# A fused decoder's last stage: TensorE transposes the probabilities ahead of the queries and keys, and GpSimd's inverse root is cut at another place

## The chip, the cores and the metric

One Trainium2 chip, one core of it. The metric is the device time of one launch in microseconds (us), the median of several runs. The kernel is written instruction by instruction: each engine (TensorE, VectorE, ScalarE, GpSimd and SyncE, which starts the transfers) has its own queue, works through it in order, and waits on semaphores that other engines raise.

## The reference, cut to what matters

The program is a decoder of four blocks, twelve parts in all, on x of shape 4 x 256 x 128. Each part adds to x what it makes of a layer norm of x. The change lies in the twelfth part, `L3_ffn`, a small transformer of its own with six layers, sixteen heads of 64 and attention in windows of 32 rows:

```python
def attn_layer(x, Wqkv, qs, ksc, Wo):
    q, k, v = split(x @ Wqkv)                   # 128 -> 3 * 1024
    q = l2norm(q) * qs;  k = l2norm(k) * ksc    # per head: t / max(norm, 1e-12)
    q = q * cos * scale + rotate_half(q) * sin * scale
    k = k * cos * inv + rotate_half(k) * sin * inv
    out = local_attention(q, k, v)              # softmax over 64 or 96 keys of a window
    return out @ Wo
def ffn_layer(x, g, b, W1, b1, W2, b2):
    xn = (x - mu) / sqrt(var + 1e-05) * g + b
    a, gate = split(xn @ W1 + b1)
    return a * gelu(gate) @ W2 + b2
for i in range(6):
    x = attn_layer(shift_tokens(x), ...) + x
    x = ffn_layer(shift_tokens(x), ...) + x
```

## The kernel before

The last stage is one block of code, `stream`, that overlaps everything. A **job** is one layer for one of the four batches: 24 jobs. A job has eight **groups**, each a pair of heads: 192 groups. Time goes in **ticks**, `for s in TICKS`, one group per tick. Every engine's queue is written as such a loop, and in tick `s` each does for the group `g = s - lag` (or `s + lead`) what its stage of the pipeline asks for. So the order of the work is fixed by where a step stands in the body of the loop, and by its lag.

In one tick TensorE does, in this order:

- one or two of the q, k and v products of a later job, 128 x 512 each (L2078, or L2087 and L2091);
- the scores of group `s` (L2100 lays the window's mask, L2108 multiplies). They wait for the turned queries and keys, `net_qk_T`, and for the exponentials of the group before;
- the **turn** (L2120): four transposes of `net_rope`, the queries and keys of group `s + 1`, into a bank of PSUM. It waits until GpSimd has scaled them (L2348), and until the turn before has been copied;
- the **flip** (L2129): four transposes of the probabilities of group `s - 2`. It waits until GpSimd has divided them by their sums (L2335), and until the flip before has been copied;
- a step that comes once a job (output projection L2141, shifts L2151 to L2153 and L2161, the feed-forward part L2170 to L2207);
- the values (L2226): probabilities of group `s - 3` times v.

VectorE, per tick: the reciprocal of the sums of group `s - 1` (L2405), the maxima of the scores of group `s` (L2409), two products of the rotation (L2373, L2379) that read a bank of PSUM, the copy of the flip (L124, `net_probs_turned`), and in odd ticks the copy of the turn (L124, `net_qk_T`; ScalarE has the even ones). In even ticks it sums squares (L2445) after the flip's copy. Once a job there are the layer norm's sums, its root (L2391 to L2399) and two residual adds (L2453, L2487). ScalarE does the exponentials, squares and further copies.

GpSimd, per tick: it divides the probabilities of group `s - 1` (L2335), scales group `s + 2` with its head norms (L2348), and adds the two products of the rotation (L2327). TensorE's flip and turn of one tick thus wait for the same tick of GpSimd, the flip for its first operation, the turn for its second.

Every four ticks comes the inverse root of the head norms, `inverse_root`: fourteen operations on 128 x 32 numbers (a start value of two operations, three Newton steps of four), each waiting for the one before it. It is cut in two lots. The **early** lot, `EARLY_OPS` operations, stands at the end of one tick (`PROJ + 5`), after the add. The **late** lot stands in the next tick (`PROJ + 6`) between the division of the probabilities and the scaling that uses its result:

```python
if j is not None:
    inverse_root(pool, head_sums[:, j % 2, :], 1e-24, head_inv[:, j % 2, :], head_temp, rooted, ROOT_OPS * j, False)
g = s + SCALE
if 0 <= g < G:
    ...
    pool.wait_ge(rooted.sem, rooted.at(0, ROOT_OPS * (j + 1)))
```

Twice in a job there is such a pair of lots. Once a layer GpSimd also makes the tables of the next layer (L2315, L2319).

## Time and profile before

| what | us |
|---|---|
| median of three runs | 2811.66 (2810.72 to 2820.9) |
| the profiled execution, its own time | 2823.85 |
| its span, first to last instruction | 2822.1 |
| busy: TensorE, VectorE, ScalarE, GpSimd | 2514.6, 1779.7, 1535.3, 1364.0 |
| the last stage, about | 1811 to 2820 |
| from one job to the next inside it | 39.83 (40.61 where a layer begins) |

The profiled execution took 12 us more than the median of the others. In the last stage TensorE is busy for 765.19 us of the 800 us from 1909 to 2709, at the full granted clock (1.00); GpSimd for 638.83 us, VectorE for 639.19 us, ScalarE for 567.11 us. The page's chain of work that ended last has 21% of the span on TensorE, 8% on GpSimd and 4% on VectorE. A job is the unit to read: all of them from the second on look alike to within some hundredths of a microsecond.

### The profile page before, as it was taken

The numbers are of one execution on the slowest core, as the hardware profiler recorded it, in microseconds if no ns is written. First come the engines' busy times: TensorE is split into PE (matmuls) and PEld (weight loads), VectorE is DVE, ScalarE is ACT, GpSimd is POOL, SyncE is SP. The second block draws the span as 40 slices with busy tenths as digits, with TensorE's granted clock in tenths as the row PEclk, the third lists the DMA queues.
The fourth block names the chain that finished last, engine by engine and source line by source line (L and its number), as shares of the span: only waits on it lengthen the run. The fifth ranks groups of instructions, "written<-read, shape, count | busy, mean of one in ns | idle before, by whom it ended". The sixth has DMA issues, their size and how long they took to land. (4 is left out here: it accounts for less than half of the span.)

```text
span 2822.1 us, 57927 instructions
## 1 busy us (share of the span) xinstructions
PE 2514.6 (89%) x20585; PEld 1603.7 (57%) x20585; DVE 1779.7 (63%) x4074; ACT 1535.3 (54%) x4979; POOL 1364.0 (48%) x1981
## 2 busy tenths in 40 slices
PE   6899978988989988978559999789999999999997
PEld 3555544645655655645444555356666666666665
DVE  4566665545656755555564555577887787878784
ACT  1455534722756755633224555357766776777664
POOL 0344442401536633320003444388877887788772
PEclk8899997998998999999768999899999999999998
DMA  3000000010000010000010000101010101101000
GB/s 71 1 1 1 1 9 1 2 34 15 2 5 1 2 34 1 1 7 1 8 29 1 1 1 1 55 17 39 20 47 20 35 24 32 35 24 47 20 26 7
DMA packets 45711, 47.85 MB, mean 17 GB/s; under 512 B 11947, under 2 KB 31413, under 8 KB 45430
## 3 DMA queue, kind: packets, MB, share of 16 engines
q1 hardware_dynamic: 45430, 44.18, 5.7%
q8 instruction: 167, 2.74, 0.4%
q14 instruction: 114, 0.93, 0.1%
HBM read 31.05 MB, written 0.52 MB: 11 GB/s over the span
## 5 line engine op out<-in xcount | busy, mean ns | idle before, releaser
L1033 DVE TENSOR_REDUCE negmax<-scores 128x1 f32<-128x508 f32 (+4 forms) x512 | 212.5, 467 | 213.8 <-PE scores L918 182.6
L1013 POOL TENSOR_TENSOR l_xattn_probs<-l_xattn_probs,rowinv 128x512 f32<-128x512 f32 x128 | 130.4, 1040 | 421.1 <-DVE rowinv L1025 421.1
L2273 ACT ACTIVATE net_probs<-bank,net_negmax 128x96 f32<-128x96 f32 x768 | 251.7, 341 | 105.1 <-DVE net_negmax L2409 104.0
L1013 POOL TENSOR_TENSOR lora_probs<-lora_probs,rowinv 128x508 f32<-128x508 f32 (+1 forms) x256 | 149.6, 618 | 247.3 <-DVE rowinv L1025 247.3
L2327 POOL TENSOR_TENSOR net_rope<-net_rope,net_sin_parts 128x512 f32<-128x512 f32 x192 | 244.7, 1274 | 10.5 <-DVE net_sin_parts L2379 10.5
L2335 POOL TENSOR_TENSOR net_probs<-net_probs,net_inverse 128x384 f32<-128x384 f32 x192 | 159.0, 828 | 140.1 <-DVE net_inverse L2405 140.1
L2348 POOL TENSOR_TENSOR net_rope<-net_rope,net_head_inv 128x512 f32<-128x512 f32 x192 | 201.5, 1050 | 7.5 <-POOL net_head_inv L1880 0.9
L124 DVE COPY turned<-flip 128x512 f32<-128x512 f32 (+3 forms) x280 | 163.1, 583 | 66.4 <-PE flip L945 52.3
L739 DVE TENSOR_REDUCE negmax<-scores 128x2 f32<-128x256 f32 (+2 forms) x192 | 157.7, 822 | 71.4 <-PE scores L647 42.0
L918 PE MATMUL scores<-kT,qM 64*128 64x512 f32 (+2 forms) x768 | 191.2, 575 | 6.1 <-ACT kT L122 2.5
L986 ACT ACTIVATE lora_probs<-scores,negmax 128x508 f32<-128x508 f32 (+1 forms) x256 | 117.8, 472 | 139.9 <-DVE negmax L1033 139.0
L2409 DVE TENSOR_REDUCE net_negmax<-bank 128x4 f32<-128x384 f32 x192 | 106.3, 554 | 133.0 <-PE bank L2108 130.9
L122 ACT ACTIVATE turned<-flip 128x512 f32<-128x512 f32 (+3 forms) x280 | 143.6, 513 | 63.2 <-PE flip L661 53.1
L968 PE MATMUL heads<-turned,V 128*64 128x256 f32 (+1 forms) x1280 | 167.4, 383 | 2.0 <-ACT turned L122 1.3
L2120 PE MATMUL bank<-ident,net_rope 128*128 128x128 f32 x768 | 126.3, 287 | 40.4 <-POOL net_rope L2348 40.4
L986 ACT ACTIVATE l_xattn_probs<-scores,negmax 128x512 f32<-128x512 f32 x128 | 86.9, 684 | 136.5 <-DVE negmax L1033 136.5
L2273 ACT ACTIVATION_READ_ACCUMULATOR net_probs<-bank,net_negmax 128x1 f32 x768 | 156.6, 204 | 0.0
L2237 ACT ACTIVATE net_squares<-bank 128x512 f32<-128x512 f32 x192 | 115.3, 600 | 69.2 <-PE bank L2078 54.9
L724 POOL TENSOR_TENSOR cross_probs<-cross_probs,rowinv 128x1024 f32<-128x1024 f32 x64 | 119.9, 1894 | 66.2 <-DVE rowinv L734 66.2
L124 DVE COPY net_probs_turned<-bank 128x512 f32<-128x512 f32 x192 | 130.9, 682 | 15.1 <-PE bank L2129 13.4
L2373 DVE TENSOR_TENSOR net_rope<-bank,net_cos_table 128x512 f32<-128x512 f32 x192 | 130.9, 682 | 11.2 <-ACT net_squares L2237 9.9
L122 ACT ACTIVATE net_rope<-bank 128x256 f32<-128x256 f32 x192 | 75.3, 392 | 111.9 <-PE bank L2226 111.2
(435 smaller groups left out, 6508.4 us busy)
## 6 DMA issues: line engine op xcount, KB each, us to landing
net_w_qkv<-in_L_ffn_Wqkv SPq DMA_DIRECT2D x12, 768.0 KB, 6.0
net_vals_between<-net_vals SPq DMA_DIRECT2D x48, 192.0 KB, 2.5
net_w_out<-in_L_ffn_Wo SPq DMA_DIRECT2D x6, 512.0 KB, 4.2
net_vals_between<-net_vals SPq DMA_DIRECT2D x48, 64.0 KB, 2.0
moe_w<-in_L_ffn_w13T SPq DMA_DIRECT2D x8, 256.0 KB, 2.8
net_w<-in_L_ffn_W SPq DMA_DIRECT2D x6, 341.0 KB
moe_w<-in_L_ffn_w2T SPq DMA_DIRECT2D x8, 128.0 KB, 2.3
ctx_tok<-in_ctx SPq DMA_DIRECT2D x1, 768.0 KB, 6.6
```

Source lines behind the costliest of these rows:

```text
L122: return nc.scalar.activation(dst, src, ACT.Copy, scale=scale)
L124: return nc.vector.tensor_copy(dst, src)
L739: nc.vector.tensor_reduce(negmax[:, c:c + 2], scores[:, 2 * half:2 * half + 2, 0:nk], AX.X, ALU.max, negate=True).then_inc(maxed.sem, 1)
L918: last = nc.tensor.matmul(scores[:, 2 * qt + h, 0:nk], qM[rows, 0, t * P:(t + 1) * P], kT[rows, k0:k0 + nk], start=True, stop=cross)
L968: last = nc.tensor.matmul(heads[rows, q0 * P:QT * P], V[:, v0 + j, rows], turned[:, 2 * p + h, c0:c0 + w], start=(j == 0), stop=(j == part ...
L986: last = nc.scalar.activation(pr[:, slot(g, qt, h), k0:k1], scores[:, 2 * qt + h, k0:k1], ACT.Exp, bias=negmax[:, u * tail + w:u * tail + ...
L1013: last = nc.gpsimd.tensor_tensor(own, own, rowinv[:, u * tail + w:u * tail + w + 1].to_broadcast([P, k1 - k0]), ALU.mult)
L1033: last = nc.vector.tensor_reduce(negmax[:, u * tail + w:u * tail + w + 1], scores[:, 2 * qt + h, k0:k1], AX.X, ALU.max, negate=True)
L2273: last = nc.scalar.activation(prob_blocks(g)[:, w, :], score_blocks(g)[:, w // 2, w % 2, :], ACT.Exp, bias=maxima[:, g % 4, w:w + 1], accu ...
L2327: nc.gpsimd.tensor_tensor(own, own, sin_parts[:, (2 * u + s) % 4, :], ALU.add).then_inc(added.sem, 1)
L2335: nc.gpsimd.tensor_tensor(prob_blocks(g), prob_blocks(g), part, ALU.mult).then_inc(shared.sem, 1)
L2348: nc.gpsimd.tensor_tensor(own, own, factor.to_broadcast([P, 4, 2, DH]), ALU.mult).then_inc(scaled.sem, 1)
```

## The change

Two edits. On TensorE the block of the flip is moved, unchanged, from behind the turn to ahead of it. In GpSimd's `inverse_root` the cut moves from behind the sixth operation to behind the eighth: the first two operations of the second Newton step (`y * y`, and times `half`) leave the late lot and end the early one. For this `newton` is split into `newton_first` and `newton_last`. No operation is added or removed.

```diff
-        EARLY_OPS, ROOT_OPS, ROOT_MAGIC = 6, 14, float(0x5F3759DF - (1 << 30) - (1 << 22))
+        EARLY_OPS, ROOT_OPS, ROOT_MAGIC = 8, 14, float(0x5F3759DF - (1 << 30) - (1 << 22))
...
-            def newton(to, last=False):
+            def newton_first(last=False):
                 then(nc.gpsimd.tensor_tensor(t, y, y, ALU.mult))
-                then(nc.gpsimd.tensor_tensor(t, t, half, ALU.mult))
+                then(nc.gpsimd.tensor_tensor(t, t, half, ALU.mult), last)
+
+            def newton_last(to, last=False):
                 then(nc.gpsimd.tensor_scalar(t, t, 1.5, None, ALU.add))
                 then(nc.gpsimd.tensor_tensor(to, t, y, ALU.mult), last)
             if early:
...
-                newton(y, last=True)
+                newton_first()
+                newton_last(y)
+                newton_first(last=True)
                 assert done[0] - before == EARLY_OPS
             else:
                 pool.wait_ge(step.sem, step.at(0, done[0]))
-                newton(y)
-                newton(out, last=True)
+                newton_last(y)
+                newton_first()
+                newton_last(out, last=True)
...
+                        g = s - FLIP
+                        if 0 <= g < G:
+                            pe.wait_ge(shared.sem, shared.at(0, g + 1))
+                            until(pe, moved, g)
+                            for w in range(BLOCKS):
+                                c0 = turned_from(w)
+                                last = nc.tensor.transpose(flip_bank[:, w * P:(w + 1) * P], probs[:, g % 3, c0:c0 + P], ident[:, :])
+                            last.then_inc(flipped.sem, 1)
                         g = s + TURN
...
-                        g = s - FLIP
-                        if 0 <= g < G:
-                            pe.wait_ge(shared.sem, shared.at(0, g + 1))
-                            until(pe, moved, g)
-                            for w in range(BLOCKS):
-                                c0 = turned_from(w)
-                                last = nc.tensor.transpose(flip_bank[:, w * P:(w + 1) * P], probs[:, g % 3, c0:c0 + P], ident[:, :])
-                            last.then_inc(flipped.sem, 1)
```

TensorE's queue in a tick with the output projection, before (L2120 is the turn, L2129 the flip):

```order
L2100 MATMUL bank<-net_window,ident 64x192 x4
L2108 MATMUL bank<-net_qk_T 64x64 x2
L2108 MATMUL bank<-net_qk_T 64x96 x6
L2120 MATMUL bank<-ident,net_rope 128x128 x4
L2129 MATMUL bank<-ident,net_probs 128x128 x4
L2141 MATMUL bank<-net_w_out,net_rope 128x128 x16
L2226 MATMUL bank<-net_probs_turned,net_vals 64x128 x2
```

and in the changed kernel, whose lines are numbered anew (L2124 is the flip, L2133 the turn):

```order
L2105 MATMUL bank<-net_window,ident 64x192 x4
L2113 MATMUL bank<-net_qk_T 64x64 x2
L2113 MATMUL bank<-net_qk_T 64x96 x6
L2124 MATMUL bank<-ident,net_probs 128x128 x4
L2133 MATMUL bank<-ident,net_rope 128x128 x4
L2145 MATMUL bank<-net_w_out,net_rope 128x128 x16
L2230 MATMUL bank<-net_probs_turned,net_vals 64x128 x2
```

The flip, which reads `net_probs`, has moved past the turn, which reads `net_rope`; all else stands as it did.

GpSimd's queue from inside an early lot to the end of the late lot that follows, before (L1877 to L1880 are the four operations of a Newton step, L2335 the division of the probabilities, L2348 the scaling):

```order
L1879 TENSOR_SCALAR net_head_temp<-net_head_temp 128x32
L1880 TENSOR_TENSOR net_head_temp<-net_head_temp 128x32
L2335 TENSOR_TENSOR net_probs<-net_probs,net_inverse 128x4x96
L1877 TENSOR_TENSOR net_head_temp<-net_head_temp 128x32
L1878 TENSOR_TENSOR net_head_temp<-net_head_temp 128x32
L1879 TENSOR_SCALAR net_head_temp<-net_head_temp 128x32
L1880 TENSOR_TENSOR net_head_temp<-net_head_temp 128x32
L1877 TENSOR_TENSOR net_head_temp<-net_head_temp 128x32
L1878 TENSOR_TENSOR net_head_temp<-net_head_temp 128x32
L1879 TENSOR_SCALAR net_head_temp<-net_head_temp 128x32
L1880 TENSOR_TENSOR net_head_inv<-net_head_temp 128x32
L2348 TENSOR_TENSOR net_rope<-net_rope,net_head_inv 128x4x128
```

and in the changed kernel (L1881 and L1882 are the third and fourth operation of a Newton step, L2339 the division, L2352 the scaling):

```order
L1881 TENSOR_SCALAR net_head_temp<-net_head_temp 128x32
L1882 TENSOR_TENSOR net_head_temp<-net_head_temp 128x32
L1877 TENSOR_TENSOR net_head_temp<-net_head_temp 128x32
L1878 TENSOR_TENSOR net_head_temp<-net_head_temp 128x32
L2339 TENSOR_TENSOR net_probs<-net_probs,net_inverse 128x4x96
L1881 TENSOR_SCALAR net_head_temp<-net_head_temp 128x32
L1882 TENSOR_TENSOR net_head_temp<-net_head_temp 128x32
L1877 TENSOR_TENSOR net_head_temp<-net_head_temp 128x32
L1878 TENSOR_TENSOR net_head_temp<-net_head_temp 128x32
L1881 TENSOR_SCALAR net_head_temp<-net_head_temp 128x32
L1882 TENSOR_TENSOR net_head_inv<-net_head_temp 128x32
L2352 TENSOR_TENSOR net_rope<-net_rope,net_head_inv 128x4x128
```

The division now stands behind eight operations of the root, and between it and the scaling there are six operations in place of eight.

## Rows read from the trace of the kernel before

**Rows 1.** Waits of TensorE, 1909 to 2709 us (total us, times, longest).

```profile
PE bank L2120 <- POOL net_rope L2348: 27.7, 24, 1.4
...
PE bank L2161 <- DVE xin L2487: 6.5, 20, 0.3
```

**Rows 2.** Timeline of TensorE, one job, 2229 to 2233 us: start, length, engine, line, operation, count, [idle <-releaser].

```profile
2229.54 0.66 PE L2120 MATMUL bank<-ident,net_rope 128*128 128x128 f32 x4 [1.23 <-POOL net_rope L2348]
2230.03 0.60 PE L2129 MATMUL bank<-ident,net_probs 128*128 128x128 f32 x4
2230.47 0.38 PE L2170 MATMUL bank<-ident,z 128*128 128x128 f32 x2
...
2232.44 0.28 PE L2100 MATMUL bank<-net_window,ident 64*64 64x192 bf16 x4
...
2232.98 0.65 PE L2120 MATMUL bank<-ident,net_rope 128*128 128x128 f32 x4
```

**Rows 3.** Timeline of GpSimd, the same job.

```profile
2223.91 0.25 POOL L1880 TENSOR_TENSOR net_head_temp<-net_head_temp 128x32 f32<-128x32 f32 x1
2224.87 0.83 POOL L2335 TENSOR_TENSOR net_probs<-net_probs,net_inverse 128x384 f32<-128x384 f32 x1 [0.71 <-DVE net_inverse L2405]
2225.66 0.24 POOL L1877 TENSOR_TENSOR net_head_temp<-net_head_temp 128x32 f32<-128x32 f32 x1
...
2226.31 0.29 POOL L1879 TENSOR_SCALAR net_head_temp<-net_head_temp 128x32 f32<-128x32 f32 x1
...
2228.44 1.05 POOL L2348 TENSOR_TENSOR net_rope<-net_rope,net_head_inv 128x512 f32<-128x512 f32 x1
```

**Rows 4.** Timeline of VectorE, the same job.

```profile
2218.99 0.56 DVE L2409 TENSOR_REDUCE net_negmax<-bank 128x4 f32<-128x384 f32 x1
...
2224.62 0.17 DVE L2405 RECIPROCAL net_inverse<-net_sums 128x4 f32<-128x4 f32 x1
...
2229.92 0.68 DVE L2379 TENSOR_TENSOR net_sin_parts<-bank,net_sin_table 128x512 f32<-128x512 f32 x1
2230.67 0.69 DVE L124 COPY net_probs_turned<-bank 128x512 f32<-128x512 f32 x1
2231.28 0.68 DVE L124 COPY net_qk_T<-bank 128x512 f32<-128x512 f32 x1
```

**Rows 5.** Timeline of VectorE, an earlier job at 1901 us.

```profile
1901.35 0.68 DVE L124 COPY net_qk_T<-bank 128x512 f32<-128x512 f32 x1
```

**Rows 6.** Timeline of TensorE, that earlier job.

```profile
1902.08 0.28 PE L2100 MATMUL bank<-net_window,ident 64*64 64x192 bf16 x4 [0.37 <-DVE net_qk_T L124]
```

**Rows 7.** Timeline of VectorE, inside the layer norm root.

```profile
2222.33 0.16 DVE L2394 TENSOR_TENSOR net_ln_temp<-net_ln_temp 128x2 f32<-128x2 f32 x1
...
2222.92 0.21 DVE L2394 TENSOR_TENSOR net_ln_temp<-net_ln_temp 128x2 f32<-128x2 f32 x1
```

**Rows 8.** Timeline of TensorE, the job where a layer begins.

```profile
2327.68 0.65 PE L2120 MATMUL bank<-ident,net_rope 128*128 128x128 f32 x4 [0.71 <-POOL net_rope L2348]
```

**Rows 9.** Timeline of TensorE, the first job.

```profile
1852.68 0.79 PE L2129 MATMUL bank<-ident,net_probs 128*128 128x128 f32 x4
1853.41 0.70 PE L2226 MATMUL bank<-net_probs_turned,net_vals 128*64 128x128 f32 x4
...
1887.48 0.66 PE L2120 MATMUL bank<-ident,net_rope 128*128 128x128 f32 x4 [1.86 <-POOL net_rope L2348]
```

**Rows 10.** Timeline of TensorE, the last job.

```profile
2751.86 0.28 PE L2100 MATMUL bank<-net_window,ident 64*64 64x192 bf16 x4 [0.56 <-DVE net_qk_T L124]
...
2766.02 1.06 PE L2129 MATMUL bank<-ident,net_probs 128*128 128x128 f32 x4
2766.88 5.77 PE L2141 MATMUL bank<-net_w_out,net_rope 128*128 128x128 f32 x32
```

**Rows 11.** Timeline of VectorE, the last job.

```profile
2778.04 0.69 DVE L124 COPY net_probs_turned<-bank 128x512 f32<-128x512 f32 x1 [0.45 <-PE bank L2129]
```

**Rows 12.** Timeline of ScalarE, the same middle job.

```profile
2234.97 0.61 ACT L122 ACTIVATE net_qk_T<-bank 128x512 f32<-128x512 f32 x1
```

## The prediction

> **What bounds the kernel now.** I read four views in this order: the busy shares, the chain of work that ended last, the waits by engine, and then the timelines of the four engines through one job. The last stage is all that changes. There TensorE is nearly dense, so a gain can only come out of TensorE's idle time, and the first thing to see is how little there is. Over 800 us, twenty jobs of 39.83 us (0.78 more where a layer begins), TensorE waits for GpSimd's scaling 24 times for 27.7 us, and for VectorE's residual add 20 times for 6.5 us [rows 1]. The second kind comes ahead of both edits and stays. The first kind is the change's place: once in each job the turn L2120 stands 1.23 us idle, and four times more where a layer begins.
>
> The turn with that wait starts at 2229.54 [rows 2]. It is released by the scaling at 2228.44 [rows 3], 1.10 us after the scaling's start. The scaling stands behind the late lot, the late lot behind the division at 2224.87, and the division waited 0.71 us for the reciprocal at 2224.62 [rows 3, 4]. So the stall's cause is VectorE, which comes late to this reciprocal because the layer norm's root and two adds fall into these ticks. From the maxima at 2218.99, which start as TensorE's scores end, VectorE runs without a pause to the rotation's product at 2229.92. Its next copies, flip at 2230.67 and turn at 2231.28, are the end of that stretch [rows 4]. Behind them TensorE's next scores start at 2232.44 [rows 2].
>
> That second fact decides how much the change can give: **two chains** reach these scores, one by GpSimd and the turn, one by VectorE alone, and the second is only a little shorter.
>
> **The flip ahead of the turn.** The four transposes take 0.44 us of TensorE (2230.03 to 2230.47). TensorE is free 1.23 us ahead of 2229.54, so at 2228.31 [rows 2]. The probabilities that the flip needs are divided at 2224.87 + 0.83 = 2225.70 [rows 3], long before. So the flip fills 0.44 of the 1.23 us, and all behind the turn could come 0.44 earlier. In ticks without a stall the two only change places: the sum on TensorE is the same, the turn ends 0.44 later and the flip about half a us earlier. VectorE copies the flip first, so this order suits it.
>
> **Eight operations in the early lot.** Two operations leave the late lot: the third operation starts 0.65 us after the first (2225.66 to 2226.31), so the scaling starts at 2227.79 and the turn can start at 2228.89. They come in behind the operation at 2223.91, where GpSimd waits 0.71 us for the reciprocal anyway: 0.65 fits in, by 0.06 [rows 3]. In the other pair of lots of a job there is no such wait: the division comes 0.65 later and the scaling at the same time as before. The flip that reads it stands two to three us behind, so I cost this at nothing; without that cover it would be up to 0.65 per job, 16 us over 24 jobs.
>
> **Both, on TensorE.** Flip from 2228.31 to 2228.75, turn at 2228.89, so 0.65 earlier; what follows the turn comes 0.65 + 0.44 = 1.09 earlier, and the next scores could start at 2232.44 - 1.09 = 2231.35.
>
> **What is late next.** The scores also need the copy of the turn. VectorE's product at 2229.92 is followed by the flip's copy 0.75 later. Two such instructions back to back are 0.61 apart (2230.67 to 2231.28) [rows 4], so 0.14 to 0.15 was waiting for the flip. With the flip long done, its copy starts at 2230.52 and the turn's at 2231.12. Where the scores waited for exactly this copy, they started 0.73 after it (1901.35 to 1902.08) [rows 5, 6]. So the scores start at 2231.85. **VectorE holds them, and the job gains 0.59 us, not 1.09.** From there on every engine moves along with TensorE until the next job's stretch.
>
> Why 0.59 and not another value: below is 0.15, if VectorE's stretch grew by as much as 0.44; above is 1.09, if the copy did not hold. The rows of this very place give 0.59, and there are 21 such stalls from 1909 to 2709 us that look alike.
>
> **A rule against it.** Two of the root's operations now lie beside VectorE's last root operations and its residual add. In the rows, the same VectorE operation, with both inputs in SBUF, takes 0.16 us once and 0.21 us some tenths later, with GpSimd at work beside it both times [rows 7]: a loss of 0.05 at most per meeting. Two meetings a job would be 0.1, or 2 us in all.
> The Trainium skill (SBUF — State Buffer, "Who interferes with whom") says that VectorE instructions with two SBUF inputs and GpSimd ones that read SBUF lock one another out for a whole instruction. By that rule two VectorE operations would stand for up to a GpSimd operation each, some 0.25 us twice per job. The trace does not show waits of that size among these operations.
> I take nothing for it in the sum, and the lock as a rival.
>
> **The sum**, in us:
>
> - 21 jobs x 0.59 = 12.4.
> - Four layer beginnings. GpSimd is busy without a pause from the stalled division through the tables, an early lot and a late lot. One late lot less, one early more, one late less: the scaling comes 0.65 earlier, and the turn at 2327.68 too [rows 8]; with the flip ahead of it, 1.09 for what follows, 0.50 more than the 0.59 already had. The output projection follows there, so no copy holds. 4 x 0.50 = 2.0.
> - First job. GpSimd is busy from its first early lot on, so only the flip counts: at half clock it takes 0.73 (1852.68 to 1853.41), and ahead of the turn at 1887.48 it takes 0.44 [rows 9]. Together 1.2.
> - Last job. The scores at 2751.86 wait for the turn's copy, which itself waited; they come 0.73 earlier. Near 2765 the scaling is 0.65 earlier and the flip, 0.86 long at the lower clock, is out of the way: 1.51, so 0.78 more [rows 10]. At 2778.04 VectorE waits 0.45 for the flip and then goes on to the layer norm's root: 0.44 more [rows 11]. Together 1.95.
>
> Sum 17.5. The profiled execution's own 2823.85 would become 2806.3 (span 2822.1 to 2804.6). Its distance to the median, 12 us, is no part of the change, so I take the sum from the median: 2811.66 - 17.5 = **2794.2 us**, 0.62% less. About 0.5%, 14 us, is what a measurement of this kernel can tell from no change.
>
> The clock is the loosest term: in the first job and twice in the last the granted clock is at its lower level (1.2 GHz) for a while after idle time, and a flip costs 0.86 there against 0.44. If such a stretch goes or moves, some 2 to 3 us come or go. With the 2 us above, the likeliest case's own range is 2789 to 2799.
>
> **The rivals.**
>
> 1. *VectorE does not hold the scores.* For it: that chain shows no wait in the rows of before. Against: its rows are back to back, and one copy's lag of 0.73 was seen. Each of the 21 jobs would give 0.42 to 0.50 more, about 9: 2785 us. Chance 0.09.
> 2. *GpSimd's two operations are paid for by VectorE or by the division.* The cover is 0.71 for 0.65; a lock of 0.5 us per job in VectorE's root, which begins the stretch that holds the scores, or a division later by as much, leaves 0.1 of 0.59. Then 12.4 falls to about 2: 2804.7 us, within 0.5%. Chance 0.17. This is also what the skill's rule gives in full.
> 3. *The change does nothing to be seen*: the wait moves whole from the turn to the scores, because another input of them (the exponentials, a product's bank) is as late as VectorE. I found none in the timelines. 2809 to 2812 us. Chance 0.03.
> 4. *Slower.* In all 192 groups the turn ends 0.44 later, with the copy and the scores of the next tick behind it. The tightest place that I found is one tick on: that turn ends at 2232.98 + 0.66, 0.44 later would be 2234.08, and ScalarE starts its copy at 2234.97, 0.9 us behind [rows 2, 12]. Only where this slack is gone does it cost; it decides from 40 ticks on (40 x 0.44 = 17.6 eats the gain), and in all 192 it would be 84 - 17 = 67 slower, 2879 us. Chance 0.03.
>
> The forecast itself has 0.68, of it 0.56 beyond the 0.5% bound (below 2797.6) and 0.12 within. So faster 0.56 + 0.09 = 0.65, same 0.12 + 0.17 + 0.03 = 0.32, slower 0.03. The range of 8 in 10 takes in the forecast and reaches to rivals 1 and 2: 2785 to 2804.
>
> **What the changed profile would show.** In a middle job the turn's wait falls from 1.23 to between 0.1 and 0.2 us, with the flip in front of it; the next scores show a new wait of 0.4 to 0.5 for `net_qk_T` of VectorE; GpSimd's division keeps less than 0.1 of its 0.71; the job takes 39.24 in place of 39.83. VectorE shows no wait for the flip. If the new wait at the scores is missing, rival 1 holds; if the job takes 39.7 and VectorE's root is longer, rival 2; if scores in other ticks wait for the turn's copy, rival 4. The prediction is wrong if VectorE's stretch from the maxima to the turn's copy, 12.1 us in the sum, measures otherwise.

## The result and the profile after

| what | before | after |
|---|---|---|
| median of nine runs each, us | 2811.81 (2810.72 to 2826.42) | 2797.31 (2791.8 to 2806.97) |
| span of the profiled execution | 2822.1 | 2791.1 |
| of it from the last stage's first matmul to the end | 1011.3 | 990.9 |
| from one middle job to the next | 39.83 | 39.25 |
| the same where a layer begins | 40.62 | 39.53 |

The ratio is 0.994, with a 95% interval from 0.9919 to 0.9961: the changed kernel is faster by 0.6%, and the predicted 2794.2 lies 3.1 us below the measured median. The two profiled spans differ by 31.0 us, twice the difference of the medians. Part of it is where the stage begins: its first matmul starts at 1810.82 in the trace of before and at 1800.20 in that of after, behind a wait of about the same length. The row of TensorE's timeline in the kernel before (start, length, engine, line, operation, count, [idle <-releaser]):

```profile
1810.82 0.66 PE L2161 MATMUL bank<-ident,xin 128*128 128x128 f32 x2 [9.38 <-PEq L1839]
```

and in the changed kernel that first matmul, the flip and the turn of the first job, the shifts L2165 (one a job) with the place of the old stall behind the first of them, and the last job's turn and output projection:

```profile
1800.20 0.66 PE L2165 MATMUL bank<-ident,xin 128*128 128x128 f32 x2 [9.59 <-PEq L1839]
...
1838.32 0.66 PE L2124 MATMUL bank<-ident,net_probs 128*128 128x128 f32 x4 [0.28 <-POOL net_probs L2339]
1841.46 0.66 PE L2133 MATMUL bank<-ident,net_rope 128*128 128x128 f32 x4 [2.49 <-POOL net_rope L2352]
...
2207.51 0.41 PE L2165 MATMUL bank<-ident,xin 128*128 128x128 f32 x2 [0.32 <-DVE xin L2491]
...
2210.90 0.66 PE L2124 MATMUL bank<-ident,net_probs 128*128 128x128 f32 x4
2211.56 0.66 PE L2133 MATMUL bank<-ident,net_rope 128*128 128x128 f32 x4
2212.12 0.44 PE L2174 MATMUL bank<-ident,z 128*128 128x128 f32 x2
...
2213.09 1.12 PE L2083 MATMUL bank<-net_w_qkv,xnT 128*128 128x512 f32 x2
2214.51 0.28 PE L2105 MATMUL bank<-net_window,ident 64*64 64x192 bf16 x4 [0.30 <-DVE net_qk_T L124]
...
2246.76 0.41 PE L2165 MATMUL bank<-ident,xin 128*128 128x128 f32 x2 [0.33 <-DVE xin L2491]
...
2286.00 0.41 PE L2165 MATMUL bank<-ident,xin 128*128 128x128 f32 x2 [0.33 <-DVE xin L2491]
...
2325.53 0.41 PE L2165 MATMUL bank<-ident,xin 128*128 128x128 f32 x2 [0.33 <-DVE xin L2491]
...
2738.53 0.66 PE L2133 MATMUL bank<-ident,net_rope 128*128 128x128 f32 x4 [0.57 <-POOL net_rope L2352]
2739.02 3.74 PE L2145 MATMUL bank<-net_w_out,net_rope 128*128 128x128 f32 x32
```

10.6 of the 31.0 us lie ahead of the stage, in code that is the same in both. In the traces of the ten experiments this start lies between 1800.97 and 1812.75, whatever the edit. So below a kernel is read first by its jobs and by its time **within the stage** (span less the start), and the medians second.

**The job.** From 2207.51 to 2246.76 is one middle job, 39.25 us; from 2286.00 to 2325.53 one in which a layer begins, 39.53 us. The wait of 0.32 for the residual add, which was there before [rows 1], is unchanged.

**Inside the job.** This job runs 17.34 us earlier than the one of [rows 2 to 4], so 17.34 is to be added for a comparison. The flip (L2124) now fills part of the stall, and the turn (L2133) has no idle time in brackets any more. It starts 0.66 after the flip, where two such blocks back to back are 0.49 apart [rows 2], so 0.17 of wait is left. The old 1.23 is gone. In its place the scores (L2105) wait 0.30 for VectorE's `net_qk_T`.

GpSimd in the same job, from the end of the early lot to the scaling:

```profile
2206.90 0.24 POOL L1877 TENSOR_TENSOR net_head_temp<-net_head_temp 128x32 f32<-128x32 f32 x1
2207.22 0.25 POOL L1878 TENSOR_TENSOR net_head_temp<-net_head_temp 128x32 f32<-128x32 f32 x1
2207.53 0.83 POOL L2339 TENSOR_TENSOR net_probs<-net_probs,net_inverse 128x384 f32<-128x384 f32 x1
...
2210.46 1.05 POOL L2352 TENSOR_TENSOR net_rope<-net_rope,net_head_inv 128x512 f32<-128x512 f32 x1
```

The two operations moved (2206.90 and 2207.22) stand where GpSimd waited 0.71 for the reciprocal [rows 3]. The division starts at 2207.53, 2224.87 on the clock of before, which is the same moment, and the scaling at 2210.46 + 17.34 = 2227.80 in place of 2228.44.

VectorE, from the reciprocal to the turn's copy:

```profile
2205.39 0.16 DVE L2400 SCALAR_TENSOR_TENSOR net_ln_temp<-net_ln_temp 128x2 f32<-128x2 f32 x1
...
2207.28 0.17 DVE L2409 RECIPROCAL net_inverse<-net_sums 128x4 f32<-128x4 f32 x1
...
2212.58 0.68 DVE L2383 TENSOR_TENSOR net_sin_parts<-bank,net_sin_table 128x512 f32<-128x512 f32 x1
2213.18 0.68 DVE L124 COPY net_probs_turned<-bank 128x512 f32<-128x512 f32 x1
2213.78 0.68 DVE L124 COPY net_qk_T<-bank 128x512 f32<-128x512 f32 x1
```

The product at 2212.58 is the one of 2229.92 in [rows 4], at the same moment; the flip's copy follows it 0.60 later in place of 0.75, and the scores start 0.73 after the turn's copy (2213.78 to 2214.51).

Waits over the stretch 1895 to 2690 us (engine, what, waits for whom: total us, times, longest):

```profile
PE bank L2165 <- DVE xin L2491: 6.5, 20, 0.3
PE bank L2105 <- DVE net_qk_T L124: 6.2, 21, 0.3
...
PE bank L2133 <- POOL net_rope L2352: 0.4, 1, 0.4
```

27.7 us of waits for the scaling [rows 1] have become 0.4 (the 0.17 a job at the turn is too short to be counted as idle), and 6.2 us for the turn's copy are new.

### The profile page after: what moved, and what is told of

Its sections match the earlier page's. It is cut to its first block and busy times, and to the rows that moved or that the text cites. A ratio compares the mean times of both kernels' runs of the same rounds, so it can differ in the third digit from the quotient of the medians.

```text
span 2791.1 us, 57927 instructions
## 1 busy us (share of the span) xinstructions
PE 2510.5 (90%) x20585; PEld 1594.0 (57%) x20585; DVE 1776.8 (64%) x4074; ACT 1530.3 (55%) x4979; POOL 1364.9 (49%) x1981
## 5 line engine op out<-in xcount | busy, mean ns | idle before, releaser
L2339 POOL TENSOR_TENSOR net_probs<-net_probs,net_inverse 128x384 f32<-128x384 f32 x192 | 158.8, 827 | 119.7 <-DVE net_inverse L2409 118.0
L2352 POOL TENSOR_TENSOR net_rope<-net_rope,net_head_inv 128x512 f32<-128x512 f32 x192 | 201.4, 1049 | 7.5 <-POOL net_head_inv L1882 0.9
L1013 POOL TENSOR_TENSOR l_attn_probs<-l_attn_probs,rowinv 128x256 f32<-128x256 f32 (+1 forms) x128 | 62.1, 507 | 139.8 <-DVE rowinv L1025 138.2
```

The source lines that it names most:

```text
L1013: last = nc.gpsimd.tensor_tensor(own, own, rowinv[:, u * tail + w:u * tail + w + 1].to_broadcast([P, k1 - k0]), ALU.mult)
L2339: nc.gpsimd.tensor_tensor(prob_blocks(g), prob_blocks(g), part, ALU.mult).then_inc(shared.sem, 1)
L2352: nc.gpsimd.tensor_tensor(own, own, factor.to_broadcast([P, 4, 2, DH]), ALU.mult).then_inc(scaled.sem, 1)
```

## The experiments

### Each edit alone: flip_only and lots_only

The edit of flip_only is the block of the flip moved as in the diff of the change, with `EARLY_OPS` left at 6; that of lots_only is the other half:

```diff
-        EARLY_OPS, ROOT_OPS, ROOT_MAGIC = 6, 14, ...
+        EARLY_OPS, ROOT_OPS, ROOT_MAGIC = 8, 14, ...
```

> The first edit alone: the flip ahead of the turn, the lots of six and eight as before. Theory (two chains, the slower sets the scores): GpSimd's scaling comes no earlier, the turn starts at the same distance from it, and only the flip's 0.44 us leave the path. A middle job takes 39.83 - 0.44 = 39.39 us, the turn's wait falls from 1.23 to about 0.8, and the scores of the next tick show no wait for VectorE's copy. In all about 12 us less than before. Rival (VectorE's end of the stretch held the scores all along, and any edit that lets it run gives the same): 39.24 us. Rival (the flip's place is worth nothing, the lots gave all): 39.83 us.

> The second edit alone: eight operations in the early lot, the flip behind the turn as before. Theory: the scaling and the turn come 0.65 us earlier, TensorE would reach the scores 0.65 earlier, VectorE's copy allows 0.59; a middle job takes 39.24 us, the same as with both edits, so that in the middle jobs the flip's place adds nothing to the lots. Where a layer begins the job gains 0.65 instead of 1.09. In all about 13 us less than before. Rival (the two edits add up in the middle jobs too): 39.83 minus what the flip alone leaves over, so 39.4 to 39.7 us. Rival (the lots give nothing, the flip gave all): 39.83 us.

TensorE's turn in a middle job of flip_only:

```profile
2215.20 0.66 PE L2128 MATMUL bank<-ident,net_rope 128*128 128x128 f32 x4 [0.64 <-POOL net_rope L2348]
```

and of lots_only, where the turn stands ahead of the flip (L2125 is the turn):

```profile
2216.59 0.66 PE L2125 MATMUL bank<-ident,net_rope 128*128 128x128 f32 x4 [0.60 <-POOL net_rope L2352]
```

| kernel | median us | ratio to the kernel before, run beside it, and interval | within the stage | job | layer job |
|---|---|---|---|---|---|
| before | | | 1011.3 | 39.83 | 40.62 |
| flip_only | 2803.28 | 0.9965 [0.9948, 0.9981] | 997.1 | 39.38 | 40.16 |
| lots_only | 2803.22 | 0.9957 [0.9941, 0.9972] | 994.2 | 39.25 | 40.00 |
| after | 2797.31 | 0.994 [0.9919, 0.9961] | 990.9 | 39.25 | 39.53 |

The flip alone gives 0.45 a job for its own 0.44, as expected. Its turn shows a wait of 0.64 where about 0.8 was expected; counted from start to start it is 0.80 (the flip ahead of it starts at 2213.91, 1.29 before the turn, where two such blocks back to back are 0.49 apart). The lots alone give 0.58, and both together also 0.58: in a middle job the flip adds nothing to the lots, since VectorE's copy holds either way. The two edits add up only where no copy holds, at the layers' beginnings: 0.46 + 0.62 = 1.08, and both give 1.09.

### VectorE's copy moved as well: turn_copy_first

The changed kernel, with one more move:

```diff
                         u = at_tick(s, PROJ + 1, 2, S)
                         if u is not None:
                             part(u, 1)
-                        g = s - FLIP
-                        ... (wait for the flip, copy it)
                         g = s + TURN
                         ... (wait for the turn, copy it)
+                        g = s - FLIP
+                        ... (wait for the flip, copy it)
```

> The changed kernel, and on VectorE the turn's copy stands ahead of the flip's copy. Theory: in the changed kernel the scores of one tick per job wait 0.30 us for this copy, at the end of VectorE's stretch; with the copy 0.60 earlier that wait goes, and a middle job takes 39.24 - 0.30 = 38.94 us, some 6 us less over the stage than the changed kernel. Rival (VectorE's copy is not what holds; GpSimd or TensorE's own work does): 39.24 us. Rival (the flip's copy is now late for something, or VectorE waits for the turn in other ticks): more than 39.24 us.

VectorE and TensorE of turn_copy_first at the same place of a job:

```profile
2212.94 0.68 DVE L2383 TENSOR_TENSOR net_sin_parts<-bank,net_sin_table 128x512 f32<-128x512 f32 x1
2213.53 0.68 DVE L124 COPY net_qk_T<-bank 128x512 f32<-128x512 f32 x1
2214.13 0.68 DVE L124 COPY net_probs_turned<-bank 128x512 f32<-128x512 f32 x1
```

```profile
2214.49 0.28 PE L2105 MATMUL bank<-net_window,ident 64*64 64x192 bf16 x4
```

The turn's copy comes right behind the product, 0.60 earlier, and the scores' wait is gone: they start 0.96 after the copy, more than the 0.73 that a held start takes. The job takes 38.86, so 0.39 less than in the changed kernel, where 0.30 was expected. From start to start the old wait was longer than the 0.30 shown: from the product ahead of the scores to the scores it is 1.42 in the changed kernel (2213.09 to 2214.51) and 1.06 here (2213.43 to 2214.49), 0.36 less. Median 2792.39 us, ratio 0.9931 [0.9912, 0.995], 987.6 us within the stage. It has the shortest job and the lowest median of the study, though the interval of its ratio overlaps that of the changed kernel. That the move of a copy on VectorE shortens the job shows that VectorE held it.

### GpSimd's cut further on: early_ten

```diff
-        EARLY_OPS, ROOT_OPS, ROOT_MAGIC = 8, 14, ...
+        EARLY_OPS, ROOT_OPS, ROOT_MAGIC = 10, 14, ...
```

(with the second Newton step whole in the early lot).

> The changed kernel with ten operations in the early lot and four in the late one. Theory: GpSimd has only 0.06 us of its wait left, so the division of that tick comes about 0.65 later, and the late lot is shorter by as much; the scaling and the turn stay where they are and VectorE holds the scores anyway, so a middle job stays at 39.24 us. The division of the other lots is 0.7 later and harms nobody. Rival (the late lot is still what bounds the job): 38.5 to 38.9 us. Rival (a late division holds up the flip, which now stands first on TensorE): more than 39.3 us.

The job is 39.25 and the scores' wait 0.30 as in the changed kernel: in a middle job the division's later start is covered, as expected. The first job shows the later division itself. The flip and the turn of that job in early_ten, for those at 1838.32 and 1841.46 in the changed kernel:

```profile
1841.54 0.66 PE L2124 MATMUL bank<-ident,net_probs 128*128 128x128 f32 x4 [1.89 <-POOL net_probs L2339]
1843.97 1.11 PE L2133 MATMUL bank<-ident,net_rope 128*128 128x128 f32 x4 [1.77 <-POOL net_rope L2352]
```

The flip waits 1.89 in place of 0.28 for the division, but the turn behind it still waits 1.77 for the scaling, so the flip's wait costs nothing. The scaling is no later for the cut: from the first operation of the root to it GpSimd takes 5.54 us in early_ten (1837.33 to 1842.87) and 5.53 in the changed kernel (1834.83 to 1840.36). No run shows a place where the later division is paid for. Within the stage 991.1 us, the changed kernel 990.9. The median, 2802.72, is higher, but here the stage began at 1804.30, 4.1 us later.

### Work added to VectorE: before_padded and after_padded

Both get two more operations on VectorE one tick behind the root, ahead of the copy of `xnT`:

```diff
+                        n = at_tick(s, LATE + 2, PER, JOBS)
+                        if n is not None:
+                            for i in range(2):
+                                nc.vector.tensor_tensor(ln_temp[:, 2, :], ln_temp[:, 1, :], ln_temp[:, 1, :],
+                                                        ALU.mult).then_inc(padded.sem, 1)
+                                dve.wait_ge(padded.sem, padded.at(0, 2 * n + i + 1))
```

> The kernel before, and on VectorE two more operations of 128 x 2, each waiting for the one before, once a job in the tick after the layer norm's root: about 0.40 us more in the stretch that ends in the copy of the turn, behind the reciprocal that GpSimd's division waits for. Nothing that is computed changes. Theory: VectorE's chain is the shorter one before the change, by 0.59 us less the 0.15 that it waits for the flip, so 0.40 fits in and a middle job stays at 39.83 to 39.9 us. Rival (VectorE holds before the change too): 40.2 us.

> The changed kernel with the same two operations more on VectorE. Theory: VectorE's chain now holds the scores, so a middle job takes 39.24 + 0.40 = 39.64 us and the wait of the scores for the copy grows from 0.30 to 0.7. Rival (the wait for the copy is only the last of several that end together, GpSimd's or TensorE's own): 39.24 us or little more.

VectorE's row of the two operations in before_padded, and GpSimd beside it:

```profile
2181.92 0.35 DVE L2474 TENSOR_TENSOR net_ln_temp<-net_ln_temp 128x2 f32<-128x2 f32 x2
```

```profile
2181.89 0.30 POOL L1880 TENSOR_TENSOR net_head_inv<-net_head_temp 128x32 f32<-128x32 f32 x1
2182.33 1.05 POOL L2349 TENSOR_TENSOR net_rope<-net_rope,net_head_inv 128x512 f32<-128x512 f32 x1
```

The same in after_padded:

```profile
2190.69 2.01 DVE L2478 TENSOR_TENSOR net_ln_temp<-net_ln_temp 128x2 f32<-128x2 f32 x2
```

```profile
2190.41 1.05 POOL L2353 TENSOR_TENSOR net_rope<-net_rope,net_head_inv 128x512 f32<-128x512 f32 x1
2191.42 1.27 POOL L2332 TENSOR_TENSOR net_rope<-net_rope,net_sin_parts 128x512 f32<-128x512 f32 x1
```

Each of the padded kernels was run once; the job is what is read. In before_padded it takes 39.87 us, as expected (2817.73 us in all, beside a median of 2816.86 for the kernel before). In after_padded it takes 41.18 where 39.64 was expected (2841.26 us). The padding itself is not 0.4 but 2.01 us long. It began while GpSimd's scaling ran, and ended at 2192.70, with the end of the add (2191.42 + 1.27 = 2192.69). In before_padded it ended at 2182.27, just ahead of the scaling. So VectorE stood still for GpSimd: one operation until the end of the scaling, the other until the end of the add. It is so in 22 of the 24 jobs; in the last two no GpSimd operation runs beside the padding, and it takes 0.34 to 0.35 us. The step of my expectation that failed is the 0.2 us for such an operation.

### What it is that stands still: after_padded_one and after_padded_recip

```diff
-  nc.vector.tensor_tensor(ln_temp[:, 2, :], ln_temp[:, 1, :], ln_temp[:, 1, :], ALU.mult)   # after_padded
+  nc.vector.tensor_scalar(ln_temp[:, 2, :], ln_temp[:, 1, :], 1.5, None, ALU.add)           # after_padded_one
+  nc.vector.reciprocal(ln_temp[:, 2, :], ln_temp[:, 1, :])                                  # after_padded_recip
```

> The changed kernel with two added VectorE operations at the place of after_padded (one tick behind the root, ahead of the copy of xnT), 128x2 as there, but each with one input in place of two; what they write is read by nobody. In after_padded the two took 2.01 us: the first ended with GpSimd's scaling, the second with the addition behind it. Theory (a VectorE operation with both inputs in SBUF stands until the running GpSimd operation ends, one with a single input doesn't): the two take about 0.4 us together though GpSimd's scaling runs beside them, the middle job takes 39.24 + 0.4 = 39.6 us, and the span is about 2791 + 21 x 0.4 = 2800. Rival (any added operation at this place waits for what the scaling works on): 2.0 us and 41.2 us a job again, as in after_padded.

The theory fell: one input, and 2.04 us all the same, job 41.20, 2849.7 us in all. The padding's row:

```profile
2197.57 2.04 DVE L2478 TENSOR_SCALAR net_ln_temp<-net_ln_temp 128x2 f32<-128x2 f32 x2
```

> The changed kernel with two added VectorE operations at the place of after_padded and after_padded_one (one tick behind the root, ahead of the copy of xnT), 128x2 and with one input as in after_padded_one, but reciprocals in place of additions of a constant; what they write is read by nobody. In after_padded_one the two additions took 2.04 us, as long as the two-input ones had, so the number of inputs is not what decides. In the trace of turn_copy_first the kernel's own reciprocals take 0.17 us with GpSimd's additions L2331 running over them from end to end. Theory A (what decides is whether the operation draws on the SBUF ports that VectorE shares with GpSimd: both one with two SBUF inputs and a constant's addition from SBUF to SBUF do, a reciprocal doesn't): the two take about 0.4 us, the job 39.24 + 0.4 = 39.6 us, the span is near 2791 + 21 x 0.4 = 2800. Theory B (the place alone: any added operation there stands behind GpSimd's scaling and addition): 2.0 us and 41.2 us a job for the third time.

VectorE, GpSimd and TensorE in after_padded_recip:

```profile
2174.34 0.36 DVE L2478 RECIPROCAL net_ln_temp<-net_ln_temp 128x2 f32<-128x2 f32 x2
```

```profile
2174.06 1.05 POOL L2353 TENSOR_TENSOR net_rope<-net_rope,net_head_inv 128x512 f32<-128x512 f32 x1
```

```profile
2178.40 0.28 PE L2106 MATMUL bank<-net_window,ident 64*64 64x192 bf16 x4 [0.59 <-DVE net_qk_T L124]
```

The reciprocals start 0.28 into the scaling and take 0.36 us together. The place is not to blame; the kind of operation is. A multiplication with two SBUF inputs and a constant's addition from SBUF to SBUF both stand until GpSimd's running operation ends; a reciprocal from SBUF to SBUF doesn't. The Trainium skill (SBUF — State Buffer, "Who interferes with whom") says just this: two SBUF inputs lay claim to the port pair shared with GpSimd, and so do copies and `tensor_scalar` where they can run in a two-port mode; whoever comes second is blocked for the whole instruction. The three traces agree (2.01, 2.04 and 0.36 us) for the case in which VectorE comes second to one of GpSimd's long operations. For a short one before_padded shows no such block: its two multiplications start 0.03 us into GpSimd's operation of 0.30 (2181.89) and take 0.35 together, as long as with no GpSimd operation beside them.

The job took 39.53 (2799.03 us in all, beside 2815.16 for the kernel before), for 39.25 + 0.36 = 39.61 at most, and the scores' wait is 0.59 in place of 0.30. This is the plain test that after_padded was meant to be: 0.36 us more on VectorE make the job 0.28 longer, while 0.35 us more in before_padded made it 0.04 longer. VectorE had room before the change and has hardly any after it.

### The root moved: root_later

turn_copy_first, and the layer norm's root stands one tick later, behind the maxima, ahead of the rotation's products (`at_tick(s, LATE + 2, ...)`).

> The changed kernel with the turn's copy first on VectorE, and the layer norm's root (twelve small operations, 2.4 us) one tick later, behind that tick's reciprocal and maxima. Theory: VectorE's stretch is as long as before, so the copy of the turn comes no sooner; but the residual add no longer stands behind the root, so TensorE's wait of 0.33 for it goes, and the reciprocal comes 2 us earlier. Then GpSimd, whose early lot of eight ends 0.1 us ahead of its old division, is what holds: the turn comes 0.1 to 0.15 earlier, and a middle job takes 38.7 to 38.8 us against 38.86 with the copy first alone. Rival (the reciprocal is what holds, and GpSimd can follow it): 38.3 us. Rival (the root's place is worth nothing, or the products of the rotation are late instead): 38.86 us or more.

VectorE's slowest root operation there, GpSimd's division beside it, and TensorE behind:

```profile
2222.36 0.75 DVE L2400 SCALAR_TENSOR_TENSOR net_ln_temp<-net_ln_temp 128x2 f32<-128x2 f32 x1
```

```profile
2222.27 0.83 POOL L2339 TENSOR_TENSOR net_probs<-net_probs,net_inverse 128x384 f32<-128x384 f32 x1
```

```profile
2225.80 1.12 PE L2096 MATMUL bank<-net_w_qkv,xnT 128*128 128x512 f32 x2 [1.90 <-DVE net_sin_parts L2383]
```

The job takes 40.59 us, 1.73 more than in turn_copy_first, and 41.76 in six of the 19 periods of the steady part. These six have a stretch at the lower granted clock: 0.50 from 2020.70 to 2024.10, in the job from 2016.57 to 2058.33, where the job after it runs at 1.00 throughout. TensorE's wait is the same 1.90 in all 19. Median 2840.3 us, ratio 1.0084 [1.0067, 1.0102]. The add's wait at the shift is gone, and in its place the last product of q, k and v (L2096) waits 1.90 for the rotation's products, which now stand behind the root. Of the root's length, 0.55 is again a stand: the operation at 2222.36 takes 0.75, where the same line takes 0.16 to 0.20 in the changed kernel, and ends with GpSimd's division (2222.27 + 0.83).

### The residual add first: add_first

turn_copy_first, and VectorE's residual add behind the down product (the block at `DOWN`, L2491) stands ahead of the root in place of behind it.

> turn_copy_first, and the residual add behind the down product stands ahead of the layer norm's root on VectorE in place of behind it. There TensorE waited 0.32 us a job for this add at the shift L2165 (20 of them), with the product already done when the root began. The wait at L2165 goes in every variant. Theory (GpSimd is the next to hold: its lots run without a pause from a division at 2202.03 to the scaling at 2210.80, the turn starts at 2211.91, 1.10 behind that, though the flip ahead of it started at 2211.26): the 0.32 comes back as a wait of the turn for the scaling, the middle job stays at 38.86 us, time the same as turn_copy_first. Rival 1 (TensorE's own work holds there): the job takes 38.5 us, 21 x 0.32 = 7 us less. Rival 2 (the root, 0.34 later, now has its last operations beside GpSimd's division and stands until it ends): job 39.2 or more.

TensorE of add_first in a middle job, from the last product to the turn:

```profile
2219.59 1.12 PE L2092 MATMUL bank<-net_w_qkv,xnT 128*128 128x512 f32 x2
2220.80 1.13 PE L2096 MATMUL bank<-net_w_qkv,xnT 128*128 128x512 f32 x2
...
2223.21 0.66 PE L2133 MATMUL bank<-ident,net_rope 128*128 128x128 f32 x4 [0.16 <-POOL net_rope L2352]
```

The shift's wait of 0.32 is gone, and the job is 38.87 us, as in turn_copy_first: the time comes back in two places. The product L2096 starts 1.21 after L2092, where 0.96 is the pitch in the changed kernel, and the turn waits 0.16 for the scaling. So the theory's result is right and its reason only half: GpSimd holds the turn, but most of the 0.32 is already caught by VectorE's rotation products, for which L2096 waits: the product of VectorE at 2220.06 is 0.74 ahead of it, the same distance as in root_later (2225.06 to 2225.80), where the wait is named. Median 2805.83 us, ratio 0.9959 [0.9945, 0.9973]. The profiled span is 15.6 us longer than that of turn_copy_first: 11.4 of it lie ahead of the stage (which starts at 1812.75 against 1801.38), 4.2 within it, behind the last middle job, where the last output projection took 6.18 us for 4.77. Whether the medians, 13.4 apart with equal jobs, differ for the same reasons is not shown.

## Why the prediction was right

**The flip fills the stall.** Right. flip_only alone gives 0.45 a job for the 0.44 taken, and in the changed kernel it stands in the old gap (2210.90).

**Two operations leave the late lot and fit into GpSimd's wait of 0.71.** Right, to 0.01: the scaling was to start at 2227.79 and did at 2227.80, the turn at 2228.89 and did at 2228.90. The division did not move. Of the 0.06 that was to be left, no wait is shown.

**VectorE holds the scores at 2231.85.** Right: 2214.51 + 17.34 = 2231.85, and VectorE's two copies stand at the 2230.52 and 2231.12 that were worked out. Its stretch from the maxima (2201.66) to the turn's copy (2213.78) takes 12.12 for the 12.1 that was named as the test. The rival that the copy doesn't hold is excluded by turn_copy_first and by after_padded_recip. One number of this step was off: the new wait shows as 0.30, not 0.4 to 0.5, so TensorE would have come at 2231.55 and not at 2231.35. From the turn to the scores it needed 2.65 where 2.90 - 0.44 = 2.46 had been reckoned. Two parts are the transposes of `z` (L2174): they start 0.56 after the turn, where the block behind the turn started after 0.49, and the values start 0.37 after them in place of 0.31. The rest is that idle time is counted from a matmul's modelled end (2213.09 + 1.12), while the product before the scores has a pitch of 1.06. It changed nothing, because TensorE was not what held.

**Rivals 3 and 4.** TensorE's only new wait is this one, once a job (the list of waits above), so no wait shows either for another input of the scores or for the turn, which ends 0.44 later in every other tick.

**The stretches of the stage**, in the profiled executions, cut at the shift's rows (steady part: 19 periods, four of them with a layer's beginning):

| stretch | before | after | difference | predicted |
|---|---|---|---|---|
| start to the first steady shift | 133.62 | 132.02 | -1.60 | -1.8 |
| steady part | 759.98 | 746.83 | -13.15 | -13.2 |
| from there to the end | 117.7 | 112.1 | -5.6 | -2.5 |

The predicted column is the sum's terms, with the jobs' 0.59 shared out (one to the first row, one to the last). In the first row, 0.2 are missing. The flip that moved ahead of the turn was to give 0.73, its length at the lower clock. But from that turn to the end of the next scores it is 4.79 us before (1852.19 to 1856.98) and 4.35 after (1841.46 to 1845.81), so it gave 0.44, and 0.1 of the 0.3 that this lacks was gained ahead of it: the granted clock is 0.50 in either kernel for a while from about the turn on, and with the flip gone from there other work ran at the lower level in its place. The flip's wait of 0.28 for the later division cost nothing, since the turn behind it waits 2.49 for the scaling. The stretch is a loose measure all the same: from the first shift to the second it takes 19.96 us before and 19.84 after, but 18.29 in before_padded, whose edit adds nothing there.

**The last stretch** is the term that was mis-sized: 5.6 for 2.5. Its first part came as reckoned: the scores of 2751.86 [rows 10] come at 2725.10, which is 1.39 earlier within this stretch (2751.86 - 2704.42 = 47.44 against 2725.10 - 2679.05 = 46.05), for 0.73 + 0.59 = 1.32. The rest, 3.0, is TensorE's clock. The output projection of the last job took 5.77 us [rows 10] and now takes 3.74 (2739.02), 2.0 less. The turn ahead of it was at the lower level too, and the block behind it started 0.91 after it (2765.11 to 2766.02), now 0.49 (2738.53 to 2739.02): 0.4 less. A second place, at 2785 in before, brings 0.6. The turn ahead of the projection, before:

```profile
2765.11 1.12 PE L2120 MATMUL bank<-ident,net_rope 128*128 128x128 f32 x4 [0.98 <-POOL net_rope L2348]
```

Both places in before, then in after (columns: us, busy time and instructions of PE, PEld, DVE, ACT, POOL, granted clock, DMA share, GB/s):

```profile
2766.00:2772.00 6.00, 6.00 (x34) 6.00 (x33) 1.29 (x2) 0.18 (x2) 0.85 (x1) 0.57 0.01 3
2785.00:2788.00 3.00, 3.00 (x36) 2.44 (x34) 1.30 (x3) 2.33 (x12) 0.43 (x1) 0.50 0.00 0
```

```profile
2739.00:2742.00 3.00, 3.00 (x29) 3.00 (x28) 0.69 (x1) 0.41 (x3) 1.27 (x2) 1.00 0.03 5
2755.00:2757.00 2.00, 2.00 (x30) 1.57 (x22) 1.25 (x2) 1.73 (x10) 0.11 (x1) 1.00 0.00 0
```

Before, both ran wholly or mostly at the lower level (1.2 GHz): 0.57 and 0.50 as means. After, both ran at 2.4 GHz. The prediction had put 2 to 3 us on the clock, as an uncertainty without a sign; in this execution it came out as 3 us of gain. No run shows that the edits brought it. The same projection takes 3.74 us in lots_only, early_ten, after_padded_recip and three more, but 4.77 in turn_copy_first, 4.98 in flip_only, 5.16 in before_padded and 6.18 in add_first. What decides the level there stays open.

**The sum and the median.** Within the stage the gain was 20.4 us for 17.5 predicted, in one pair of executions, and the clock's 3.0 is the difference; the medians moved by 14.5, the ratio's interval is 11 to 23 us. The start of the stage alone moves by up to 12 us between executions, so the agreement of the median to 3 us is in part luck, and that of the jobs to 0.01 is not.

**The lock, rival 2.** (Its own sum holds a slip: 17.5 with 12.4 fallen to 2 is 7.1, so 2804.6 and not 2804.7.) The lock was rightly left out of the forecast: in the changed kernel the root's operations are as long as before (0.16 and 0.21, [rows 7]), and from the one at 2205.39 to the reciprocal it is 1.89 us, 1.90 before. But the reason given was too weak. It rested on meetings with GpSimd's 128x32 operations, which cost at most 0.05. The trace of before also held one with a long operation, at its tail: the root's first operation (L2391, a constant's addition) starts at 2221.86, takes 0.23 us and ends 0.02 after GpSimd's rotation add (2220.80 + 1.27); in root_later, where it stands clear of that add, it takes 0.16. The padded kernels show that a meeting with a long one costs up to what is left of its length. root_later shows such a meeting in the root itself, 0.55 us with the division. Had the cut at eight put one there, it would have taken most of the job's 0.59; that is an estimate from root_later, not a run.

## What to carry to other kernels

Where one engine stalls once a period, follow the stall back and then ask which second chain reaches the same point: here the path over GpSimd and TensorE was shortened by 1.09 us and VectorE's let 0.59 through, and the next edit worth making was on VectorE (a copy moved, 0.39 more a job), not on the engine that had stalled. Two edits that fill the same stall don't add up: each alone gave 0.45 and 0.58, both 0.58. Before small VectorE operations between SBUF tensors are added or moved, look at what GpSimd runs at that moment: multiplications and constants' additions took 0.16 to 0.24 us beside short operations and up to 1.2 beside long ones, reciprocals 0.15 to 0.17 beside long ones too.

## What the runs showed of the hardware that was not expected

One line of VectorE over all 48 of its instructions, in after_padded and in after_padded_recip (duration in ns: least/median/greatest, first and last start):

```profile
L2478 DVE TENSOR_TENSOR net_ln_temp<-net_ln_temp x48: 148/790/1198, 1902.2 to 2822.6; 128x2 f32<-128x2 f32 x48
```

```profile
L2478 DVE RECIPROCAL net_ln_temp<-net_ln_temp x48: 152/162/168, 1897.7 to 2780.4; 128x2 f32<-128x2 f32 x48
```

The same place and the same size, and between the two kinds of operation a factor of up to seven. The operation itself needs 0.15 to 0.16 us (the least of both lines); the rest of the median of 0.79 is spent standing until GpSimd is done. A small effect on GpSimd was seen as well: its root operation beside the padding of before_padded took 0.30 us where 0.25 is usual.
